# Two of thirteen token tiles leave the dense sparse-layer products and are computed from gathered weight rows on VectorE

## The reference

```python
x = x + attention(layernorm(x), ctx)
x = x + ffn(layernorm(x))

def ffn(xf):                                   # (1600, 1024)
    inter = xf @ c1_w.T @ c2_w.T               # (1600, 3584), rank 16
    blk = inter.reshape(B * T, 56, 64)
    idx = jnp.argmax(blk, axis=-1) + jnp.arange(0, 3584, 64)
    w1_g, w2_g = w1[idx], w2t[idx]             # (1600, 56, 1024) each
    h = jax.nn.relu(jnp.einsum('bkm,bm->bk', w1_g, xf))
    return jnp.einsum('bk,bkm->bm', h, w2_g)
```

## Time and profile before

| | |
|---|---|
| median of 3 runs | 3780.05 us (3776.37 to 3783.52) |
| the profiled execution's own time | 3778.14 us |
| its span in the profile | 3776.5 us |
| mean granted TensorE clock | 0.982 of full speed |
| busy share of the span: PE, DVE, ACT, POOL | 95%, 55%, 38%, 16% |
| moved by DMA | 414.08 MB |

### The profile page before, as it was taken

The page is one execution under the profiler, slowest core; times in us unless marked ns, Lnnn a source line. Parts: engine busy times, 40 slices in busy tenths (PEclk is TensorE's granted clock), DMA queues, the critical chain, the costliest instruction groups (busy, mean ns, idle before and its releaser), DMA issues. The chain is left out here.

```text
span 3776.5 us, 53987 instructions
## 1 busy us (share of the span) xinstructions
PE 3592.4 (95%) x18762; PEld 3188.5 (84%) x18762; DVE 2086.1 (55%) x3570; ACT 1439.3 (38%) x2676; POOL 608.7 (16%) x901
## 2 busy tenths in 40 slices
PE   6999999899998999999998999997899999899999
PEld 5888887899998888888886886885899999788787
DVE  5555575777665777777775334333666666322422
ACT  4333343444334777777764223224111111222321
POOL 0000000000003666677661000000000000000000
PEclk8999999999999999999998999998999999999999
DMA  3333333454443333333335445443111111444543
GB/s 123 98 104 98 103 96 101 111 133 115 120 122 109 106 106 106 106 105 89 105 82 171 130 119 181 124 122 119 46 60 69 71 65 63 155 128 122 183 125 96
DMA packets 506580, 414.08 MB, mean 110 GB/s; under 512 B 174596, under 2 KB 424452, under 8 KB 506388
## 3 DMA queue, kind: packets, MB, share of 16 engines
q1 hardware_dynamic: 500964, 395.52, 36.1%
q0 software_dynamic: 4368, 14.00, 1.1%
q10 hardware_dynamic: 1056, 2.10, 0.2%
HBM read 292.85 MB, written 118.69 MB: 109 GB/s over the span
## 5 line engine op out<-in xcount | busy, mean ns | idle before, releaser
L1992 PE MATMUL wo_acc<-wo_w,wo_l 128*128 128x512 f32 (+1 forms) x2496 | 574.5, 392 | 24.3 <-DVE wo_l L1942 24.0
L426 PE MATMUL kv_bank<-kv_wo,kv_so 128*128 128x512 f32 x2436 | 574.8, 395 | 15.5 <-DVE kv_wo L518 11.2
L1992 PEld LDWEIGHTS wo_acc<-wo_w,wo_l 128*128 128x128 f32 (+1 forms) x2496 | 461.4, 185 | 137.2 <-DVE wo_w L1966 26.7
L426 PEld LDWEIGHTS kv_bank<-kv_wo,kv_so 128*128 128x128 f32 x2436 | 457.9, 190 | 110.3 <-issue 16.7
L814 PE MATMUL pr_bank<-pr_xo,pr_wp 128*128 128x400 f32 x2688 | 498.7, 347 | 29.0 <-ACT pr_s L881 13.4
L1992 PE MATMUL w_acc<-w_w,w_l 128*128 128x512 f32 (+1 forms) x2184 | 502.1, 392 | 21.2 <-DVE w_l L1942 21.2
L814 PEld LDWEIGHTS pr_bank<-pr_xo,pr_wp 128*128 128x128 f32 x2688 | 493.5, 190 | 31.8 <-DVE pr_wp L898 24.0
L26 PE MATMUL hid_acc<-x1t,hid_w 128*128 128x400 f32 x2688 | 509.6, 347 | 1.8 <-DVE hid_h L1755 1.3
L1992 PEld LDWEIGHTS w_acc<-w_w,w_l 128*128 128x128 f32 (+1 forms) x2184 | 403.5, 185 | 119.6 <-DVE w_w L1966 23.1
L26 PEld LDWEIGHTS hid_acc<-x1t,hid_w 128*128 128x128 f32 x2688 | 488.1, 189 | 2.6 <-issue 1.6
L1310 PE MATMUL outs<-pt,v 128*128 128x384 f32 (+3 forms) x1536 | 347.2, 348 | 27.7 <-DVE pt L1408 13.9
(11 more groups left out here) (171 smaller groups left out, 3804.2 us busy)
## 6 DMA issues: line engine op xcount, KB each, us to landing
wo_l_raw<-o_scratch SPq DMA_DIRECT2D x192, 256.0 KB, 2.8
w_l_raw<-h_scratch SPq DMA_DIRECT2D x168, 256.0 KB, 2.9
pair_raw<-in_L_xattn_Wq_dram SPq DMA_DIRECT2D x64, 512.0 KB, 5.9
q_scratch<-pr_out SPq DMA_DIRECT2D x128, 200.0 KB, 2.5
o_scratch<-o_stage SPq DMA_DIRECT2D x64, 400.0 KB, 3.7
q_raw<-q_scratch SPq DMA_DIRECT2D x64, 384.0 KB, 3.2
stage<-in_ctx_dram SPq DMA_DIRECT2D x45, 512.0 KB, 4.4
h_scratch<-hid_h SPq DMA_DIRECT2D x28, 800.0 KB, 3.7
```

What stands on the lines that cost most here:

```text
L426: last = pe.matmul(bank[:, BANK[i], :], so[:, i, a, c, :], wo[:, i, e, c, :], start=(not opened and c == 0 and (a, e) == PAIRS[0]), stop=( ...
L1992: last = pe.matmul(acc[p][:rows, :], l[j % 2][:, a, k, :rows], w[:, c, m * per + k, :], start=(m == 0 and k == 0 and (a, c) == PAIRS[0]), ...
```

## The change

Token tiles 0 and 1 (256 tokens) are no longer part of the two dense products of the sparse layer. They are computed from the chosen rows alone: for each of the 2 tiles and 56 groups, POOL gathers the chosen w1 rows of the 128 tokens, 4 KB each (an indirect transfer of 0.5 MB), VectorE multiplies them with the normalised tokens and sums up (`dot`), the sum is clipped at zero (`clip`), POOL gathers the chosen w2t rows, and VectorE adds them, scaled, to the tokens' result (`axpy`), which began as the residual.

- Of the 112 dot products, 26 stand in the hidden layer, one a block from the second pair on, between evacuations 0 and 1, with four gather buffers. The other 86, and the 112 additions, stand in the last product, 198 steps spread evenly over all units but the last six, with eight buffers.
- `normalise` leaves tiles 0 and 1, normalised, in two buffers that stay (`keep`).
- The hidden layer's products cover 1344 tokens, in four groups of 336; 11 masks are transposed instead of 13. The gate and the picks stay as they were, for all tokens. A small subtraction a pair turns the leading keys into row numbers (`indices`). VectorE's pairs are written out instead of looped.
- The last product is a new function, `project_down`, with no loops: 11 tiles, 154 units. SP stores the results, not POOL; the two tiles are stored at the very end. The order of its dense work is that of before.
- The semaphores of the first two stages are cleared by POOL and used again, in the output product.

```diff
-        raw = [sb(f"raw{i}", [P, hidden]) for i in range(R)]
+        ring = [sb(f"raw{i}", [P, hidden]) for i in range(R)]
+        raw = [keep[t] if t < len(keep) else ring[t % R] for t in range(NT)]
...
-                sp.dma_start(raw[t % R][:n, :], source[a:a + n, :]).then_inc(landed[t % R], 16)
+                sp.dma_start(raw[t][:n, :], source[a:a + n, :]).then_inc(landed[t % R], 16)
...
+class SparseTiles:
+    R_HIDDEN, R_DOWN, PER_PAIR = 4, 8, 2
+    def __init__(self, sem, S, groups, per, idx, keep, value, w1, w2t, residual):
+        self.S, self.groups, self.tokens = S, groups, S * P
+        self.idx, self.keep, self.value, self.w1, self.w2t, self.residual = idx, keep, value, w1, w2t, residual
+        self.gathered = [sem(f"row_gathered{i}") for i in range(max(self.R_HIDDEN, self.R_DOWN))]
+        self.done, self.clipped = sem("row_done"), sem("value_clipped")
+        dots = [("in", n % S, n // S) for n in range(S * groups)]
+        sums = [("out", n % S, n // S) for n in range(S * groups)]
+        count = self.PER_PAIR * (groups // per - 1)
+        self.hidden, late = dots[:count], dots[count:]
+        self.down = []
+        for n, step in enumerate(sums):
+            self.down += late[len(late) * n // len(sums):len(late) * (n + 1) // len(sums)]
+            self.down.append(step)
+        self.pairs = groups // per - 1
+        where = {step: k for k, step in enumerate(self.down)}
+        assert all(("in", s, g) not in where or where["in", s, g] < where["out", s, g] for _, s, g in sums)
+    def gather(self, pool, kind, s, g, row):
+        return pool.indirect_dma_start(row[:, :], None, (self.w1 if kind == "in" else self.w2t)[:, :],
+                                       bass.IndirectOffsetOnAxis(self.idx[:, s, g:g + 1], 0))
+    def column(self, s, g):
+        return self.value[:, g * self.S + s:g * self.S + s + 1]
+    def dot(self, dve, s, g, row):
+        return dve.tensor_tensor_reduce(row[:, :], row[:, :], self.keep[s][:, :], 1.0, 0.0, ALU.mult, ALU.add,
+                                        self.column(s, g))
+    def clip(self, dve, steps):
+        at = self.value[:, steps[0]:steps[-1] + 1]
+        return dve.tensor_scalar(at, at, 0.0, None, ALU.max)
+    def axpy(self, dve, s, g, row, total):
+        return dve.scalar_tensor_tensor(out=total[:, :], in0=row[:, :], scalar=self.column(s, g), in1=total[:, :],
+                                        op0=ALU.mult, op1=ALU.add)
...
+    skip = sparse.tokens
+    tokens = x1t.shape[3] - skip
...
-    parts = ((0, 8), (8, tt - 8))
+    parts = ((sparse.S, 8), (sparse.S + 8, tt - 8 - sparse.S))
...
+            pool.wait_ge(made, 2)
+            pool.iota(base, [[sparsity, sparse.groups]], base=sparsity, channel_multiplier=0,
+                      allow_small_or_imprecise_dtypes=True).then_inc(base_made, 1)
...
+            for k, (kind, s, g) in enumerate(sparse.hidden):
+                pool.wait_ge(idx_made, g // per + 1)
+                if k >= slots:
+                    pool.wait_ge(dotted, k - slots + 1)
+                sparse.gather(pool, kind, s, g, ring[k % slots]).then_inc(gathered[k % slots], 16)
...
-                        lambda a, c: x1t[:, a, c, t * width:(t + 1) * width], chunks).then_inc(summed, 1)
+                        lambda a, c: x1t[:, a, c, skip + t * width:skip + (t + 1) * width], chunks).then_inc(summed, 1)
...
+            def indices(i):
+                at = slice(i * per, (i + 1) * per)
+                dve.tensor_tensor(sparse.idx[:, :, at],
+                                  base[:, at].rearrange("q (a c) -> q a c", a=1).to_broadcast([P, sparse.S, per]),
+                                  lead[:, :sparse.S * per].rearrange("q (a c) -> q a c", a=sparse.S),
+                                  ALU.subtract).then_inc(idx_made, 1)
+            def dot(k):
+                kind, s, g = sparse.hidden[k]
+                dve.wait_ge(gathered[k % slots], 16 * (k // slots + 1))
+                sparse.dot(dve, s, g, ring[k % slots]).then_inc(dotted, 1)
...
+                    dots = [] if first else [sparse.PER_PAIR * (i - 1) + sparse.PER_PAIR // 2 * p + n
+                                             for n in range(sparse.PER_PAIR // 2)]
...
+                        if p == 0:
+                            indices(i + 1)
...
                     evacuate(i, p, 0)
+                    for k in dots[:1]:
+                        dot(k)
                     evacuate(i, p, 1)
...
+                if not first:
+                    dve.wait_ge(dotted, sparse.PER_PAIR * i)
+                    sparse.clip(dve, range(sparse.PER_PAIR * (i - 1), sparse.PER_PAIR * i)).then_inc(clipped, 1)
...
-            over_pairs(dve, body)
+            for i in range(pairs):
+                body(i, i % 2, i + 1 < pairs, i == 0)
...
+def project_down(nc, sem, left, left_stored, weights, residual, out, sparse):
...
+    order = [(h, t) for h in range(halves) for t in range(tiles)]
+    units = []
+    for h in range(halves):
+        units += [(h, t, m) for m in range(quads) for t in range(2)]
+        units += [(h, t, m) for t in range(2, tiles) for m in range(quads)]
...
+    share = len(steps) / (NU - 6)
+    take = [(int(share * u), int(share * (u + 1))) if u < NU - 6 else (len(steps), len(steps)) for u in range(NU)]
+    take[NU - 7] = (take[NU - 7][0], len(steps))
...
+        ring = [sb(f"ring{i}", [P, halves * cols]) for i in range(slots)]
+        ys = [sb(f"ys{s}", [P, halves * cols]) for s in range(sparse.S)]
...
+            for u, (h, t, m) in enumerate(units):
+                n = h * tiles + t
+                if t == 0:
+                    load_w(h * quads + m)
+                if u == 0:
+                    for before, count in left_stored:
+                        sp.wait_ge(before, count)
+                load_left(u)
+                if u == 1:
+                    for s in range(sparse.S):
+                        sp.dma_start(ys[s][:, :], sparse.residual[s * P:(s + 1) * P, :]).then_inc(x_landed, 16)
+                if m == 2:
+                    load_residual(n)
+                if m == 4 and (t >= 2 or (t == 0 and h)):
+                    if t == 2:
+                        store(n - 2)
+                    store(n - 1)
+            store(len(order) - 1)
+            for s in range(sparse.S):
+                sp.wait_ge(consumed, past + len(steps))
+                sp.dma_start(out[s * P:(s + 1) * P, :], ys[s][:, :]).then_inc(x_stored, 16)
+            for p in range(2):
+                sp.wait_ge(stored[p], 16 * (len(order) // 2))
+            sp.wait_ge(x_stored, 16 * sparse.S)
...
+        def _(pool):
+            for k, (kind, s, g) in enumerate(steps):
+                if k >= slots:
+                    pool.wait_ge(consumed, past + k - slots + 1)
+                sparse.gather(pool, kind, s, g, ring[k % slots]).then_inc(gathered[k % slots], 16)
...
+            def sparse_step(k):
+                kind, s, g = steps[k]
+                row = ring[k % slots]
+                dve.wait_ge(gathered[k % slots], 16 * (rows_in[k % slots] + k // slots + 1))
+                if kind == "in":
+                    sparse.dot(dve, s, g, row).then_inc(consumed, 1)
+                    dve.wait_ge(consumed, past + k + 1)
+                    sparse.clip(dve, range(g * sparse.S + s, g * sparse.S + s + 1)).then_inc(clipped, 1)
+                else:
+                    before = [j for j in range(k) if steps[j][0] == "out" and steps[j][1] == s]
+                    if before:
+                        dve.wait_ge(consumed, past + before[-1] + 1)
+                    else:
+                        dve.wait_ge(x_landed, 16 * sparse.S)
+                    mine = [j for j in range(k) if steps[j] == ("in", s, g)]
+                    if mine:
+                        dve.wait_ge(clipped, sparse.pairs + sum(1 for j in range(mine[0] + 1) if steps[j][0] == "in"))
+                    sparse.axpy(dve, s, g, row, ys[s]).then_inc(consumed, 1)
+            for u, (h, t, m) in enumerate(units):
+                if t == 0:
+                    g = h * quads + m
+                    for k in range(0, per, 2):
+                        dve.wait_ge(w_high, 2 * g + k // 2 + 1)
+                        low = dve.tensor_tensor(w[:, 1, m * per + k:m * per + k + 2], w_raw[g % 2][:, k:k + 2, :],
+                                                w[:, 0, m * per + k:m * per + k + 2].bitcast(F32), ALU.subtract)
+                    low.then_inc(w_low, 1)
+                dve.wait_ge(l_high, u + 1)
+                dve.tensor_tensor(l[u % 2][:, 1, :, :heights[t]], l_raw[u % 2][:, :, :heights[t]],
+                                  l[u % 2][:, 0, :, :heights[t]].bitcast(F32), ALU.subtract).then_inc(l_low, 1)
+                n = h * tiles + t
+                if (t, m) == (0, 0) and n:
+                    add(n - 1)
+                if (t, m) == (2, 0):
+                    add(n - 2)
+                if t >= 2 and m == 1:
```

(60 more changed lines are left out.)

131 lines of the change are left out of this document (121 added, 10 removed).

## The result

The changed kernel takes 3746.69 us (median of 3 runs, 3741.77 to 3751.24) against 3780.05; the ratio of the two is 0.9912, with a 95% interval of 0.9886 to 0.9937. It is faster by 33 us, where 73 were forecast (3707). The gain of the first part came as worked out (73.6 us); a loss of 45.5 us in the second, which the sum had at 3, took more than half of it.

What follows compares the result with a forecast made beforehand. TensorE, busy 95% of the span, was taken as the bound, with DMA the new narrowest place in the last product. Hidden layer -74 us and last product +3 took 3778 to 3707 us; range 3645 to 3800.

Steps and rivals of the forecast that it cites:

- the second: Last product: 76 us saved on TensorE are spent on waiting; stage 531 us against 528 before, so +3 us.
- Hidden layer, -74 us forecast: Hidden product: matmuls of 336 columns for 400 and fewer mask transposes, less 4 us; net -74 us, bounds -60 and -78.
- Rival F: Hidden product: the matmul stays at 178 ns despite fewer columns; kernel 3781 us; chance 0.03.
- The prices of the new operations: New steps on VectorE and POOL: dot and addition 1.222 us each, clip 0.154, a gather's issue about 1.2 us.
- rival E: POOL or VectorE slower than its nearest row: kernel about 3840 us, or 3751 with only the additions slower; chance 0.10.
- The start, 13 us: Last product: 13 us until TensorE starts, 10.5 before, since eight gathers and ys compete with the first weights.
- The weight phases, 127 us: Last product: 14 pairs of units that also load w2t, 2T + 3.0 = 9.1 us each, 127 us.
- The steady unit, T = 3.05 us: Last product: 120 units at 3.05 us, between 2.85 and 3.4, as gathers delay tiles loaded two units ahead; 366 us.
- rival D: Last product: tile loads queue behind gathers, landing 6.2 us, unit 3.85 us, stage 649, kernel 3825 us; chance 0.15.
- The transfers' own need, 2.85 us a unit: Last product: DMA transfers of a steady unit, 1.18 us plus 1.34 gathers of 1.25 us, ask for 2.85 us.
- Rival B, 3666 us: Last product: eight gather slots absorb every burst, all hidden; unit 2.85 us, stage 490 us, kernel 3666 us; chance 0.22.
- forecast case: Whole kernel: 3707 us, own range 3675 to 3745; chance 0.50.

Runs made afterwards that it cites:

- hidden_narrow: Changed kernel with the hidden layer's 26 dot products on 16 of 1024 columns, gathers kept: 3748.51 us.
- lraw4_per4: Changed kernel with four buffers instead of two for the loaded pieces of h, and four hidden-layer dots a pair instead of two: 3672.71 us.
- lraw4: Changed kernel with four buffers instead of two for the loaded pieces of h: 3659.41 us, ratio 0.9687 to the kernel before.
- narrow_dve: Changed kernel with the last product's dots and additions on 16 of 1024 columns, all gathers kept: 3746.29 us.
- plain_rows: Changed kernel with the last product's 198 gathers replaced by plain transfers of 128 consecutive rows of the same size: 3757.62 us.
- few_gathers: Changed kernel where, after the last product's first 8 gathers, POOL loads only 64 KB for 512 KB a step: 3651.02 us.

## Why the prediction went wrong, point by point

- **Hidden layer, -74 us forecast:** right, -73.6 measured. The matmul of 336 columns takes 152 ns (151), the block 17.55 us (17.5), VectorE comes just in time, and hidden_narrow and lraw4_per4 show both sides of that edge. Rival F is out.
- **The prices of the new operations:** dot 1.219 us and 0.08 us for reading out its accumulator (1.222), addition 1.280 (1.222), clip 0.154, POOL's gather 0.94 to 1.4 (1.2). All near; rival E is out. The Trainium skill (Vector Engine (DVE) Microarchitecture Reference, "Points that are easy to get wrong") halves the throughput of the scalar-tensor-tensor form with two SBUF sources that aren't bf16. By that rule the addition would take about 2.3 us, an estimate from the 1.22 us of a 1024-element product and the 0.69 of a 512-element one; the runs show 1.28.
- **The start, 13 us:** 14.5 (3171.38 to 3185.89). **The weight phases, 127 us:** 124 (3185.9 to 3249.6, and 3468.9 to 3529.1). Both right.
- **The steady unit, T = 3.05 us:** this is the term that failed. It is 3.46; 120 x 0.41 = 49 us, which is the whole miss of the stage but for small terms (573.6 for 531). The mechanism was named: issue, landing and 1.4 us of ScalarE and VectorE in two units. What was mis-sized is the landing in it: T = 3.05 leaves a piece 2 x 3.05 - 1.4 = 4.7 us, between one gather in the way (4.15) and two (5.4). The median landing is 5.1 us, and the relation gives (5.1 + 1.4) / 2 = 3.25 for it, but the late ones (6.6 and 8.0 us in the chain above) are not made good by the early ones, since there is no third buffer. The effective landing is 2 x 3.46 - 1.4 = 5.5, near the 5.6 us that the loads on the chain take in the mean, and what two gathers in the way would have given. It is just short of the 5.6 at which rival D takes the whole gain. The truth lay between forecast and D.
- **The transfers' own need, 2.85 us a unit:** too high, by a little. A busy share of 0.43 at 122 GB/s had stood for a full rate of 284 GB/s for 512-byte rows. lraw4 carried the full mix in 2.76 us a unit, at 375 GB/s, next to TensorE's 2.72. So the transfers' throughput did not set the pace of 3.46; how much more than 375 GB/s the engines would carry of this mix, no run shows. Of the signs named, the copy's wait for its load came, the landing was a little over its 4 to 5 us, and the low parts came 3.45 us apart, between the forecast's 3.05 and D's 3.5. The forecast named a DMA share under 0.8 as its refutation; the share came out at 0.91, which lraw4 shows to be no proof of a limit.
- **Rival B, 3666 us:** refuted for this kernel. Eight slots for the gathers don't help a piece of h that has two. With four for the pieces its number comes about (3659), with a steady unit of 2.76 us for B's 2.85.
- **Sums of the prediction that don't come out:** the transfers of a pair of units in the weight phase are 1.57 MB at 252 / 0.83 = 304 GB/s, 5.2 us and not 4.75, which puts B at 3672; D's landing of 6.2 us gives T = 3.80 and not 3.85 (3817 us); POOL at 3.3 us a gather gives 3829 and not 3841, both VectorE operations at 2.44 us 3830. None of these is a term of the forecast.
- **The chances:** 3746.7 us lies a hair above the forecast case's own range (3675 to 3745) and inside 3645 to 3800, on the side that was called likely. The size was wrong: 33 us of gain for 73.

## What to carry to other kernels

When a change puts a bulk stream on the DMA engines, ask first of the stream that was there before how far ahead it is loaded, and size that by the tail of its landing time beside the new traffic, not by its median alone. Here two buffers more of 2 KB a partition shortened the stage by 85 us, 71 of them by taking back what the new stream had cost, about twice the gain that the change had brought without them. And a busy share of the DMA engines near 0.9 in a stage that waits for loads is no proof of a full pipe: try a deeper ring before taking bytes away.

## What the runs showed of the hardware

- The busy share of the DMA engines doesn't add up to a rate: 0.43 at 122 GB/s before, 0.91 at 301 GB/s with waits in it, 1.04 at 375 GB/s without.
- POOL's gather of 128 rows takes 0.94 us where VectorE's steps are short and 1.2 to 1.4 us beside full ones. narrow_dve, and lraw4, both from 3260 to 3440 us:

```profile
L1542 POOL DMA_INDIRECT w_ring<-in_L_ffn_w2t_dram,idx x39 | 36.7, 941 | 62.8 <-DVE value L1549 48.6 <-DVE w_ys L1557 8.5 <-issue 5.7
```

```profile
L1539 POOL DMA_INDIRECT w_ring<-in_L_ffn_w2t_dram,idx x47 | 67.1, 1429 | 31.7 <-DVE value L1546 14.2 <-issue 9.1 <-DVE w_ys L1554 8.4
```

  The Trainium skill (SBUF — State Buffer, "Who interferes with whom") has a VectorE instruction with two SBUF inputs contend with a GpSimd instruction that reads SBUF; the rows agree in direction. The plain transfers of plain_rows, beside full-width steps too, take 0.53 us on POOL, as those of few_gathers do (0.54), so it is the gather alone that gets longer. VectorE's side shows nothing of it: the additions take 1.28 us in few_gathers and plain_rows as well, where POOL issues no gather in that stretch. It cost nothing here, since POOL had room (115 of 180 us busy in lraw4).
- Plain 0.5 MB transfers of neighbouring rows slow the pieces of h as much as gathers do (3.57 against 3.45 us a unit, in one execution each).
